# Attention on one Trainium2 core: the values' operand from a second, column-wise copy of the context; roots by one power; low parts of k a tile later, in halves

## The reference, cut to what matters

```
def _layernorm(x): return (x - mean(x)) / sqrt(var(x) + 1e-5)
# x and ctx_2048: (4, 512, 512); 8 heads of ch = 64 rows each
def _L0_xattn_ref(q, k, v):
    qh, kh, vh = (t.reshape(bs * 8, ch, 512) for t in (q, k, v))
    attn = softmax(einsum('bct,bcs->bts', qh * scale, kh * scale))
    return einsum('bts,bcs->bct', attn, vh)
x = x + tanh(g_xattn[0]) * _L0_xattn_ref(_layernorm(x), ctx_2048, ctx_2048)
x = x + tanh(g_ffn[0]) * _L0_ffn_ref(_layernorm(x), w_gate, ...)   # top 2 of 8 experts
```

## Time and profile before

| | |
|---|---|
| median of 3 runs | 1229.34 us (1228.84 to 1230.68) |
| the profiled execution, first to last instruction | 1221.8 us |
| busy in it: PE, DVE, POOL, ACT | 1070.8, 706.4, 600.0, 494.6 us |
| attention, first scores to the last product with values | 28.9 to about 330 us |
| mean granted TensorE clock | 0.957 of 2.4 GHz |

### The profile page before, as it was taken

One profiled execution on the slowest core, in us unless ns is written; L12 is line 12 of the kernel. 1 busy time (PEld: TensorE's weight loads), 2 busy tenths in 40 slices (PEclk: granted clock), 3 DMA queues, 4 the chain that ended last, 5 costly groups with the idle time before them and its releaser, 6 DMA issues. The chain is left out here.

```text
span 1221.8 us, 19314 instructions
## 1 busy us (share of the span) xinstructions
PE 1070.8 (88%) x5503; PEld 752.8 (62%) x5503; DVE 706.4 (58%) x1598; ACT 494.6 (40%) x874; POOL 600.0 (49%) x742
## 2 busy tenths in 40 slices
PE   3999989899856999999788989999997999999930
PEld 2555555555425777777358748677586777788720
DVE  4678888878524888888377616546231333343426
ACT  2565555655404888888433022212211222222200
POOL 5465555656433666666542555647250434343530
PEclk9999999999987999999899989999998999999975
DMA  9854356534165333333440212022025999899739
GB/s 309 298 193 142 135 191 226 183 117 153 63 212 180 100 108 104 103 104 102 168 152 6 78 55 83 26 80 75 5 67 207 365 347 312 279 309 352 199 73 365
DMA packets 115968, 202.39 MB, mean 166 GB/s; under 512 B 19847, under 2 KB 28039, under 8 KB 115898
## 3 DMA queue, kind: packets, MB, share of 16 engines
q1 hardware_dynamic: 95802, 167.47, 40.0%
q0 software_dynamic: 20096, 34.08, 10.0%
HBM read 133.36 MB, written 87.03 MB: 180 GB/s over the span
## 5 line engine op out<-in xcount | busy, mean ns | idle before, releaser
L1959 POOL DMA_INDIRECT sums<-summary,m_token x64 | 99.1, 1549 | 163.2 <-DMA sums<-summary,m_token 81.3
L973 POOL TENSOR_TENSOR m_down_lo<-wo,m_down_hi 128x512 fp32r<-128x512 f32 x80 | 133.3, 1686 | 80.7 <-ACT m_down_hi L1048 80.7
L491 PE MATMUL bank<-win,vT 128*128 128x512 f32 x256 | 124.1, 597 | 0.0
L661 DVE TENSOR_REDUCE negmax<-bank 128x1 bf16<-128x512 f32 x128 | 86.9, 679 | 38.8 <-PE bank L498 38.4
L584 ACT ACTIVATE win<-bank 128x512 f32<-128x512 f32 x128 | 69.4, 594 | 97.3 <-PE bank L483 95.1
L1062 DVE TENSOR_TENSOR m_up_lo<-w,m_up_hi 128x1024 fp32r<-128x1024 f32 x80 | 99.2, 1240 | 10.2 <-ACT m_up_hi L1035 8.4
L1272 POOL DMA_INDIRECT tab<-stage_up,slot x64 | 66.4, 1038 | 50.7 <-DVE slot L1607 32.5
L498 PE MATMUL bank<-k_hi,q_parts 128*128 128x512 f32 x128 | 70.8, 553 | 23.2 <-DVE q_parts L739 14.5
L1982 PE MATMUL bank<-y,m_w 128*128 128x128 f32 x736 | 89.7, 275 | 0.0
L1982 PEld LDWEIGHTS bank<-y,m_w 128*128 128x128 f32 x736 | 86.4, 193 | 0.5 <-issue 0.5
L2137 PE MATMUL bank<-w_sd,stage_gate 128*128 128x512 f32 x192 | 84.9, 598 | 0.3 <-DVE stage_gate L2127 0.3
(11 more groups left out here) (289 smaller groups left out, 2481.6 us busy)
## 6 DMA issues: line engine op xcount, KB each, us to landing
tab<-zeros SPq DMA_DIRECT2D x16, 1056.0 KB
m_w<-in_L_ffn_Wg SPq DMA_DIRECT2D x46, 256.0 KB
m_w<-in_L_ffn_Wu SPq DMA_DIRECT2D x46, 256.0 KB
m_w<-in_L_ffn_Wd SPq DMA_DIRECT2D x46, 256.0 KB
m_x<-tab SPq DMA_DIRECT2D x40, 256.0 KB, 2.6
ytab<-m_y SPq DMA_DIRECT2D x40, 256.0 KB, 2.0
stage_up<-tab SPq DMA_DIRECT2D x32, 264.0 KB
m_x<-tab SPq DMA_DIRECT2D x32, 264.0 KB
```

Of the source, the lines that this page charges most:

```text
L491: nc.tensor.matmul(pO[s * 2 + h][:], vT[:, s, sb_, h:h + 2, :].rearrange("p a c -> p (a c)"), probs[:, sb_ % 2, h, :], start=(sb_ == 0), s ...
L661: nc.vector.tensor_reduce(negmax[:, s, m:m + 1], pM[:], AX.X, ALU.max, negate=True).then_inc(pm_read, 1)
L973: nc.gpsimd.tensor_tensor(dn_lo[:, m, :], row(wo0, e * MB + m), dn_hi[:, m, :], ALU.subtract).then_inc(dn_lo_ready, 1)
L1959: nc.gpsimd.indirect_dma_start(T["sums1"][e % SUMS], bass.IndirectOffsetOnAxis(token[:, e % META:e % META + 1], 0), y[:, e % RING, :], Non ...
```

## The change

- A second copy of the context is passed in from outside the kernel, `in_ctx_by_column`, laid out as tile, column within a block of 128, head, block, row of the head. `load_v` loads a tile of it into `vT` with two DMAs; one run in memory is 64 floats (256 bytes) in SBUF, 1024 runs a tile. The eight transposes, the two copies by ScalarE, and the waits on `vT_full` and `vT_ready` are gone. TensorE waits for `v_loaded` in block 1 instead.
- SyncE loads v of tiles 0 and 1 behind k of tiles 0 and 1. In the loop `load_v(t)` stands behind `load_k(t)`, behind a wait for all products of tile t - 2 (`p_used` at 8(t - 1)), which owned the slot.
- The guess and the Newton steps are replaced by one GpSimd instruction, `pow` with exponent -0.5. VectorE only adds epsilon.
- `k_lo` of tile i + 1 is made in GpSimd's step i (before: tile i + 2), one half ahead of the multiplication by the reciprocals and one behind the addition to x.

```diff
+        def load_v(eng, t, slot):
+            src = A["ctx_by_column"][t] if isinstance(t, int) else \
+                A["ctx_by_column"][bass.ds(t, 1)].rearrange("o p h s c -> p (o h) s c")
+            for h in range(2):
+                eng.dma_start(vT[:, slot, :, 2 * h, :], src[:, h]).then_inc(v_loaded[slot], 16)
...
             for t in range(2):
                 load_k(sp, t, t)
+            for t in range(2):
+                load_v(sp, t, t)
             sp.dma_start(x_sb[:, NA:, :], x_v[:, NA:, :]).then_inc(s_xB, 16)
...
-                    sp.wait_ge(vT_full, t - 1)
                     sp.wait_ge(k_lo_ready, t - 1)
                     load_k(sp, t, n)
+                    sp.wait_ge(p_used, u * 16 + (n * 8 - 8))
+                    load_v(sp, t, n)
                 behind(u)
...
+            def low_half(k, h):
+                s = k % 2
+                pool.wait_ge(k_hi_ready, k + 1)
+                last = nc.gpsimd.tensor_tensor(k_lo[:, s, h, :], kd[:, s, h, :], k_hi[:, s, h, :], ALU.subtract)
+                if h:
+                    last.then_inc(k_lo_ready, 1)
...
-                    for _ in range(3):
-                        newton(nc.gpsimd, pool, rstd[:, a:z], ve[:, a:z], nt[:, a:z])
+                    nc.gpsimd.tensor_tensor(rstd[:, a:z], ve[:, a:z], power[:, a:z], ALU.pow)
+                    pool.drain()
...
                     if b == 1 and valid(i):
                         need(pe, po_read, i - 1)
-                        need(pe, vT_ready, i + 1)
+                        pe.wait_ge(v_loaded[s], u * 32 + 32)
...
-                    if b == 1 and valid(i + 1):
-                        for t in range(4):
-                            for h in range(2):
-                                last = nc.tensor.transpose(pT[:, t * P + h * HEAD:t * P + h * HEAD + HEAD],
-                                                           kd[0:HEAD, o, h, t * P:t * P + P], ident[0:HEAD, 0:HEAD])
-                        last.then_inc(vT_full, 1)
...
-                    if b == 2 and valid(i + 1):
-                        need(act, p_used, i * 8)
-                        need(act, vT_full, i + 2)
-                        pv = pT[:].rearrange("p (t a c) -> p t a c", t=4, a=2)
-                        nc.scalar.copy(vT[:, o, :, 0, :], pv[:, :, 0, :])
-                        nc.scalar.copy(vT[:, o, :, 2, :], pv[:, :, 1, :]).then_inc(vT_ready, 1)
...
-                        rsqrt_guess(nc, dve, rstd[:, a:z], mv[:, a:z, 1], half[:, a:z], ve[:, a:z]).then_inc(guess_ready, 1)
+                        nc.vector.tensor_scalar(ve[:, a:z], mv[:, a:z, 1], LN_EPS, None, ALU.add).then_inc(var_ready, 1)
```

More of the change, by code:

```diff
@@ L239, in attention @@
         rstd = sb("rstd", [P, 2])
-        half, ve, nt = sb("half", [P, 2]), sb("ve", [P, 2]), sb("nt", [P, 2])
+        ve, power = sb("ve", [P, 2]), sb("power0", [P, 2])
         ln1 = sb("ln1", [P, 2, 2])
@@ L375, in _ @@
             nc.gpsimd.memset(wsel[:], 0.0)
+            nc.gpsimd.memset(power[:], -0.5)
             nc.gpsimd.iota(iota_e[:], [[1, E1]], base=0, channel_multiplier=0, allow_small_or_imprecise_dtypes=True)
@@ L405, in _ @@
                                             ALU.mult, ALU.add).then_inc(q_ready, 1)
+                if valid(i + 1):
+                    low_half(i + 1, 0)
                 if valid(i - 1):
@@ L417, in _ @@
                     a, z = cols[0], cols[-1] + 1
-                    pool.wait_ge(guess_ready, i + 4)
-                    for _ in range(3):
-                        newton(nc.gpsimd, pool, rstd[:, a:z], ve[:, a:z], nt[:, a:z])
+                    pool.wait_ge(var_ready, i + 4)
+                    nc.gpsimd.tensor_tensor(rstd[:, a:z], ve[:, a:z], power[:, a:z], ALU.pow)
+                    pool.drain()
                     for n, ln in ((0, ln2[:, (i - 1) % 2]), (1, ln1[:, (i + 3) % 2])):
@@ L430, in _ @@
                     pool.drain()
[L431 to L435, removed]
-                    for h in range(2):
-                        last = nc.gpsimd.tensor_tensor(k_lo[:, s, h, :], kd[:, s, h, :], k_hi[:, s, h, :], ALU.subtract)
-                    last.then_inc(k_lo_ready, 1)
+                    nc.gpsimd.engine_nop().then_inc(ln_done, 1)
             for s in range(2):
@@ L532, in step @@
                             need(pe, k_hi_ready, i + 2)
[L533 to L537, removed]
                         rough(i + 1, o, (0, 2, 4, 7)[b])
@@ L550, in step @@
                         last.then_inc(xnT_full, 1)
-                    if b == 1 and valid(i + 1):
-                        for t in range(4):
-                            for h in range(2):
-                                last = nc.tensor.transpose(pT[:, t * P + h * HEAD:t * P + h * HEAD + HEAD],
-                                                           kd[0:HEAD, o, h, t * P:t * P + P], ident[0:HEAD, 0:HEAD])
-                        last.then_inc(vT_full, 1)
                     if b == 2 and valid(i - 2):
-                        need(pe, vT_ready, seen(i + 1))
                         need(pe, xnT_ready, i - 1)
@@ L2169 @@
         A[name] = nc.dram_tensor(f"in_{name}", a.shape, mybir.dt.from_np(a.dtype), kind="ExternalInput").ap()
+    turned = arrays["in_ctx_2048"].reshape(TILES, 2, HEAD, TPB, P).transpose(0, 4, 1, 3, 2)
+    arrays["in_ctx_by_column"] = np.ascontiguousarray(turned)
+    A["ctx_by_column"] = nc.dram_tensor("in_ctx_by_column", turned.shape, F32, kind="ExternalInput").ap()
     out = nc.dram_tensor("out", inputs["x"].shape, mybir.dt.float32, kind="ExternalOutput").ap()
```

40 lines of the change are left out of this document (6 added, 34 removed).

## The result

The changed kernel takes 1229.84 us (median of 20 runs, 1227.08 to 1234.35). The kernel before, on the same chip, takes 1226.96 us (20 runs, 1224.65 to 1232.51). The ratio is **1.0027, interval 1.0016 to 1.0038**: slower by 2.9 us. The forecast was slower by 24.7 us (1254 against 1229.34). The profiled execution has a span of 1225.7 us (before 1221.8) and a mean granted clock of 0.951 (before 0.957).

The account below looks back on a forecast made before the run. TensorE's order was taken to set the time, with even tiles of k now stalling it behind SyncE's queue. Span 1221.8 - 22.6 gain + 45 stalls + 2 for tile 2 = 1246.2, plus 7.5 to the median: 1254 us, range 1228 to 1275.

Parts of the forecast that it names:

- the stall of an even tile of k: SyncE's queue: even k lands behind `behind`, so TensorE stalls; 7.5 us per even tile (bounds 4.5 and 10), 45 us for six.
- the gain: Split of q, transposes and roots: 1.4 us a step over 14 steps, plus head and end, 22.6 us.
- the 2 us for tile 2: Tile 2 of k, issued behind `behind(0)` as before, has 0.5 MB of v more ahead: 2 us, bounds 0 and 4.
- the wait is short: Rival: `behind` moves in 12 us, not 16.7, k lands at S + 21, stall 2 to 4 us; 1229 us, chance 0.05.
- k at S + 25.7: Landing of an even tile of k, counted from S, the step's first scores matmul; wanted at S + 17.3.
- Stall 5.5: TensorE's block 1 after an even tile's late k starts at S + 28.3 instead of S + 22.8: 5.5 us.
- VectorE's lag +1: After the late k, VectorE's reciprocals start late and hold up rough m = 2 and 3 by about 1 us more.
- clock +1: TensorE's granted clock falls to the lower level behind the gap: 1 us per even tile, bounds 0 and 3.
- A wait of 0.96 us: TensorE's first rough matmul waits 0.96 us a step for the split of q; all of it was counted as gained.
- Head and end: Faster roots: 1 us at the head of the pipeline, 2 us at the end, where context weighting starts earlier.
- The loads slip past: Rival: DMA engines serve k beside `behind`, k lands by S + 17, the gain is all there; 1207 us, chance 0.13.
- GpSimd late as well: Rival: first half of `k_lo` and VectorE's reciprocals exclude each other, x comes 1.3 us later; 18 us more, 1272 us, chance 0.15.

Follow-up runs that it names:

- k_first: Changed kernel, but SyncE issues the next even tile of k ahead of the 4.7 MB of weights and zeros (`behind`): 1198.35 us, 0.9783 of the kernel before.
- no_drain: Changed kernel with GpSimd's drain between multiplication and addition to x replaced by a semaphore: 1231.85 us, 1.0041 of the kernel before.
- warm: Changed kernel with two extra TensorE matmuls of 512 columns ahead of rough 0 in every second step: 1225.92 us, 1.0016 of the kernel before.
- roots_halves: Kernel before with the power for the roots and k_lo in halves a tile later, values loaded and turned as before: 1203.25 us, 0.9839.
- values_no_drain: Kernel before with only the values' operand changed, k ahead of weights and zeros, and a semaphore for GpSimd's drain: 1219.58 us, 0.9973.

## Why the prediction was right and wrong

Sign and place were right, the size was not: +24.7 us were forecast, +2.9 came. The step that failed is the stall of an even tile of k, put at 7.5 us and 45 in all, where the runs show 5.3 and about 30. A second term, the gain, was too small: 22.6 us where 27 came. These two make up 19 of the 22 us, and the 2 us for tile 2, of which little is seen, nearly the rest. That the time fell on the 1229 us of the rival "the wait is short" is luck: neither term was that rival's.

**The stall, 45 us for six tiles, was about 30.** `k_first` against the changed kernel is 29.9 us, and 5.3 us a pair (40.7 - 35.4) where the sum had 7.5. Going through the step:

- k at S + 25.7: it came at S + 23.8, 1.9 us earlier. `behind` began at S + 5.0 and not 5.5. From there to the cast the working had 20.2 us: 16.7 of `behind`, v's bytes (+1), k's own bytes and landing (+2.5). It took 18.8 (186.46 to 205.28). In the trace all of these bytes lie in one stretch that ends at about 204.2, 17.7 us after `behind` is begun, so the two small loads and the landing added 2.1 us to the 16.7 and not 3.5.
- Stall 5.5: in `no_drain`, where nothing else is in the way, TensorE waits 4.44 us in the pair shown, 4.7 at most. In the changed kernel 1.83 us show as a wait for k. The rest: the new gap makes the odd step begin 1.9 us later (S + 19.2, in `no_drain` S + 17.4), and k is cast 0.8 us earlier in its step (S + 23.8 against 24.6).
- VectorE's lag +1 and clock +1: together 0.9 (5.3 less 4.4), because they overlap, as `warm` showed. The bound 0 of the clock was the better value.
- Tile 2: ScalarE waited 2.03 us, as forecast; without that wait the time is the same within the intervals (0.9775 against 0.9783), so of the 2 us in the sum little or nothing is seen.

**The gain, 22.6 us, was about 27.** Steps of `k_first` and of before, by block (starts of the scores in the timelines of PE):

| block | before, S = 177.94 | k_first, S = 164.32 | gained | forecast |
|---|---|---|---|---|
| 0 | 5.54 | 4.19 | 1.35 | 0.96 |
| 1 | 4.46 | 3.71 | 0.75 | 0.64 |
| 2 | 4.54 | 5.13 | -0.59 | -0.4 |
| 3 | 4.77 | 4.39 | 0.38 | 0.2 |
| step | 19.31 | 17.42 | 1.89 | 1.4 |

Block 0 of before, where the earlier trace rows leave it out, and then of `k_first` (timelines of PE):

```profile
179.35 0.62 PE L483 MATMUL bank<-identb,negmax 128*128 128x128 bf16 x8 [0.23 <-DVE negmax L661]
...
183.48 0.48 PE L474 MATMUL bank<-q_parts,k_hi 128*128 128x512 f32 x1
```

```profile
164.32 0.50 PE L456 MATMUL bank<-q_parts,k_hi 128*128 128x512 f32 x1 [0.18 <-issue]
...
167.52 0.79 PE L480 MATMUL bank<-k_hi,q_parts 128*128 128x512 f32 x1
...
168.51 0.48 PE L456 MATMUL bank<-q_parts,k_hi 128*128 128x512 f32 x1
```

Each line has the sign that was forecast; most of the surplus is in block 0. A wait of 0.96 us was taken as 0.96 us of gain. Before, the scores follow the rough matmul by 0.70 us (182.78 to 183.48), and the wait begins where the last product ends. Without the wait the rough matmul starts at 167.52, while the last products (166.12 for 1.96 us) still run, and the scores stand 0.99 us behind it, most of it beside them. The 0.23 us that TensorE waited for the last rough maximum is smaller too. Over 14 steps the table is worth 7 us more than the sum had, which is more than the 4 us to be explained. It is of one step of each kernel; the pairs (39.05 to 39.3 and 35.4) give 1.8 to 1.95 a step, but not all steps do: `k_first` still has the wait for tile 2 and one gap of 2.24 us. Head and end came as in the sum: the first rough matmul stands at 15.36 (before 16.43), and the weighting of the context follows the start of the last product after 2.33 us (before 4.63).

By whole runs the surplus seems to lie elsewhere: `roots_halves` gave 19.7 us where its terms sum to 19.2, and from there to `k_first` it is 6.9 us, where the values' operand was to give 3.4. One pair of steps of `roots_halves` (S = 186.37 and 205.12) shows why. Its step without the drain's gap has blocks of 4.21, 4.45, 4.53 and 4.32, together 17.51: all but 0.09 us of what `k_first` has, and block 0 as short. Its step with the gap takes 18.75, where `k_first`, which has the gap in one step only, takes 35.4 - 17.42 = 18.0. So in this pair the surplus is that of the split and the roots, the values' operand gave 0.7 us in block 1 and lost nearly all of it in block 2, and most of the way from `roots_halves` to `k_first` is the gap's. No run of `roots_halves` without the drain confirms it.

**The rivals.** "The loads slip past" did not happen: k waits until the queue ahead of it is empty. "The wait is short" had its time right (1229 us) and its reason wrong: `behind` did not move in 12 us, it took the time of the earlier trace rows. "GpSimd late as well" was right for another reason than the one weighed. The reciprocals kept 1753 ns beside the first half of `k_lo` (1263 to 1298 ns), so that cover held. GpSimd became late through its drain, which the prediction did not look at: `behind` moved forward in the step, and it asked only who stands behind it in SyncE's queue, not whose transfers run beside it. In this kernel that cost was hidden.

**Short runs.** The loads of an odd tile of k follow v in the queue. Issued between 165 and 170 us they took this long to land, where the earlier trace rows have 2.6:

```profile
DMA to landing us min/median/max: 3.8/3.9/4.1
```

Part of that is v's own bytes. Nothing waits for it, and `values_no_drain` gains what was computed without such a cost. The Trainium skill, page "DMA: Bandwidth & Descriptors", section "Specifications", asks for 512 bytes a run for line rate; no row here separates its rate from the rest.

## What to carry to other kernels

When a wait is put into a DMA queue, write down for every load behind it the bytes that are now ahead and the latest time at which it is wanted: up to that time lateness is free (3 us here, at most), beyond it the wait sets the pace, and what the other engines lose in the same stretch costs nothing in turn. Put the load that is wanted next ahead of the bulk that is not. Where an engine has transfers of its own under way, order its instructions by a semaphore and not by a drain. Before a stall is added to other waits in a sum, ask whether they lie inside it; and price a wait on TensorE by the distance between the block's starts, not by the idle time in its bracket.

## What the runs showed of the hardware

- Between two instructions of GpSimd a drain stood for 0.32 us when the packets of its own indirect DMAs had ended. When they had not, which was where they shared the DMA engines with the 4.7 MB, it stood until 0.5 to 1.0 us after the last of them, gaps of 0.5 to 3.8 us. With a semaphore set by the instruction ahead it was 0.08 us, with packets still to come.
- A reciprocal of 128x256 on VectorE (1.75 us) and GpSimd's subtraction of 128x512 (1.27 us) do not slow each other. The split of q (0.69 us alone, 1.66 beside `k_lo`) and the mask of 128x8 (0.17 us alone, 1.24 beside it) are slowed.
- The power on GpSimd took 0.55 us and more for 128x1 and 0.72 us for 128x2.
- The granted clock was 0.50 at 208 to 211, behind 205 to 207, where TensorE was busy for 0.34 of 2 us, and stayed at 1.00 when 1.88 us of matmuls stood in that pause (`warm`).
